# Four groups of SBUF tiles start at another byte of their 128-byte line

## The reference

```python
# layer 0, three rounds: gated recurrent update
a_in = a_out = adj @ h;  av = concat(a_in, a_out)
z = sigmoid(lin(av, w3) + lin(h, u3));  r = sigmoid(lin(av, w4) + lin(h, u3))
hv = tanh(lin(av, w5) + lin(r * h, u5));  h = (1 - z) * h + z * hv
# layer 1: attention without softmax
q, k, v = x @ Wq.T, x @ Wk.T, x @ Wv.T
rel = adjacency.T * (q @ k.T);  rel = rel / norm(rel, axis=2);  out = rel @ v
# layer 2
out = (adj @ x) @ weight + bias
# layer 3, norm_adj = adj scaled by the inverse roots of its row sums on both sides
out = norm_adj @ (x @ weight) + bias
```

## The kernel before, in words

| byte in the line | tiles |
|---|---|
| 0 | w34T, w4T, w5T, u3T, u5T, wvT, wqk, ident, adj_nat; all of the states hf and hb; all of both lanes (a, gate, rh, z, kept, cand); x_front, input_t |
| 32 | adjT, norm_adjT, w2s, w3s, sum, rel (an empty tile of 32 bytes, `shift_32`, stands ahead of them) |
| 64 | normed, result, v, sq_sum (behind `shift_back`) |

## Time and profile before

### The profile page before, as it was taken

The page is one execution under the profiler, slowest core; times in us unless marked ns, Lnnn a source line. Parts: engine busy times, 40 slices in busy tenths (PEclk is TensorE's granted clock), DMA queues, the critical chain, the costliest instruction groups (busy, mean ns, idle before and its releaser), DMA issues.

```text
span 1212.9 us, 21243 instructions
## 1 busy us (share of the span) xinstructions
PE 1198.3 (99%) x7454; PEld 1079.2 (89%) x7454; DVE 1002.6 (83%) x2220; ACT 655.7 (54%) x1179; POOL 191.7 (16%) x447
## 2 busy tenths in 40 slices
PE   9999999999999999999999999999999999999997
PEld 8789899898988989899898998989889898998896
DVE  7689788897878879788897888978789797885898
ACT  5455555555555555555555555555555555554442
POOL 1002021110211203012020211102111030120022
PEclk9999999999999999999999999999999999999998
DMA  6030221303113030220302213031130302200001
GB/s 209 18 88 18 70 71 35 104 0 88 50 35 104 0 104 35 52 87 14 107 17 69 69 35 104 0 87 52 35 104 0 104 35 51 87 12 24 1 2 35
DMA packets 105021, 66.93 MB, mean 55 GB/s; under 512 B 65690, under 2 KB 98468, under 8 KB 104996
## 3 DMA queue, kind: packets, MB, share of 16 engines
q1 hardware_dynamic: 104784, 66.08, 18.2%
q0 software_dynamic: 192, 0.52, 0.2%
q10 hardware_dynamic: 20, 0.01, 0.0%
HBM read 35.13 MB, written 23.07 MB: 48 GB/s over the span
## 4 chain that ended last, share of the span: by engine, by line
PE 97%; DVE 2%; POOL 0%; ACT 0%; issue 0%; DVEq 0%; POOLq 0%
PE b_ps L520 41%; PE f_ps L520 32%; PE f_ps L515 15%; PE b_ps L515 7%; PE f_ps L682 1%; PE b_ps L746 1%; PE b_ps L564 0%; PE f_ps L1057 0%; DVE f_stats L1683 0%; DVE hf_feat L1699 0%; DVE f_gate L1699 0%; DVE b_rh_lo L1725 0%; PE b_ps L579 0%; DVE b_ps L1720 0%; PE f_ps L589 0%
## 5 line engine op out<-in xcount | busy, mean ns | idle before, releaser
L428 POOL TENSOR_TENSOR b_var_eps<-b_moments,eps 128x2 f32<-128x2 f32 x120 | 34.7, 289 | 904.2 <-DVE b_moments L1690 904.2
L1120 ACT ACTIVATE f_cand<-f_ps,bias_c 128x512 f32<-128x512 f32 x66 | 45.4, 689 | 85.2 <-PE f_ps L520 85.2
L430 POOL TENSOR_TENSOR b_rstd<-b_var_eps,neg_half 128x2 f32<-128x2 f32 x120 | 88.0, 733 | 9.4
L1068 ACT ACTIVATE b_rh_hi<-b_ps 128x512 fp32r<-128x512 f32 x90 | 53.6, 596 | 63.0 <-PE b_ps L520 62.9
L1108 ACT ACTIVATE f_gate<-f_ps,bias_r 128x512 f32<-128x512 f32 x66 | 45.3, 686 | 71.0 <-PE f_ps L520 71.0
L1068 ACT ACTIVATE b_a_hi<-normed 128x512 fp32r<-128x512 f32 x60 | 37.8, 630 | 60.0 <-DVE normed L1699 60.0
L520 PE MATMUL f_ps<-adjT_hi,hf_node_hi 128*128 128x256 f32 x264 | 66.4, 285 | 0.0
L520 PE MATMUL f_ps<-adjT_lo,hf_node_hi 128*128 128x256 f32 x264 | 65.0, 280 | 0.0
L1582 DVE TENSOR_TENSOR f_cand<-f_z,f_cand 128x512 f32<-128x512 f32 x66 | 45.4, 688 | 23.0 <-ACT f_cand L1120 22.9
L1725 DVE TENSOR_TENSOR b_rh_lo<-b_ps,b_rh_hi 128x512 fp32r<-128x512 f32 x90 | 61.1, 679 | 4.0 <-ACT b_rh_hi L1068 3.9
L1566 DVE TENSOR_TENSOR f_gate<-f_gate,hf_feat 128x512 f32<-128x512 f32 x66 | 44.7, 678 | 20.0 <-ACT f_gate L1108 20.0
(11 more groups left out here) (340 smaller groups left out, 4304.4 us busy)
## 6 DMA issues: line engine op xcount, KB each, us to landing
x_front<-in_x SPq DMA_DIRECT2D x16, 512.0 KB, 3.9
x_blocks<-in_x SPq DMA_DIRECT2D x60, 128.0 KB, 2.9
input_t<-hf_feat SPq DMA_DIRECT2D x15, 512.0 KB, 3.0
turn_sum<-normed SPq DMA_DIRECT2D x14, 512.0 KB, 2.7
result<-turn_sum SPq DMA_DIRECT2D x56, 128.0 KB, 2.9
turn_f<-f_gate SPq DMA_DIRECT2D x14, 512.0 KB, 2.7
f_z<-turn_f SPq DMA_DIRECT2D x56, 128.0 KB, 2.8
out<-result SPq DMA_DIRECT2D x14, 512.0 KB, 3.2
```

Source lines behind the costliest of these rows:

```text
L428: pool.tensor_tensor(Y.var_eps[:, g], Y.moments[:, g, :, 1], eps[:], ALU.add).then_inc(Y.s_var, 1)
L430: pool.tensor_tensor(Y.rstd[:, g], Y.var_eps[:, g], neg_half[:], ALU.pow).then_inc(Y.s_rstd, 1)
L1068: return act.activation(dst, src, ACT.Copy)
L1120: act.activation(L.cand[:, k], L.ps1[:, k], ACT.Tanh, bias=bias_c[:, k:k + 1]).then_inc(L.s_tanh, 1)
```

## The change

Empty tiles of 64 bytes ([P, 16] in float32) are allocated ahead of four pairs of tiles, and another 64 bytes behind each pair. The pairs are: `rh_hi`, `rh_lo` of each lane, `wvT_hi`, `wvT_lo`, and the four tiles of `w2s` and `w3s`. So rh and wvT start at byte 64 of a line (before: 0), w2s and w3s at byte 96 (before: 32). All other tiles keep their byte within the line, though those behind a pair stand 128, 256, 384 or 512 bytes further on. No instruction is added, removed or reordered; nothing reads or writes the empty tiles.

```diff
@@ class Lane
         self.gate = sb(f"{name}_gate", full)
+        sb(f"{name}_half_line", [P, 16])
         self.rh_hi, self.rh_lo = sb(f"{name}_rh_hi", full, F32R), sb(f"{name}_rh_lo", full, F32R)
+        sb(f"{name}_half_line_back", [P, 16])
         self.z = sb(f"{name}_z", full)
@@ build
         u5T = split_matrix("u5T")
+        sb("half_line_v", [P, 16])
         wvT = split_matrix("wvT")
+        sb("half_line_v_back", [P, 16])
         wqk = split_matrix("wqk")
@@ build
         norm_adjT = split_matrix("norm_adjT")
+        sb("half_line_w", [P, 16])
         w2s = split_matrix("w2s")
         w3s = split_matrix("w3s")
+        sb("half_line_w_back", [P, 16])
```

## The result

The change makes the kernel slower. The median of its 4 runs is 1226.38 us (1225.23 to 1226.55); the kernel before, run beside it, had 1214.81 (1214.09 to 1216.31). The ratio is 1.0094, 95% interval 1.0079 to 1.0109: 11.6 us, or 0.95%. The forecast was 1213.8 us with a range up to 1218.2, so the result lies outside the range, on the side that had 0.15.

The account below looks back on a forecast made before the run. TensorE was taken as the bound, computing for 99% of the span. Terms -0.97 + 0.13 + 0 + 0 = -0.84 us took 1214.77 to 1213.93, against the median 1213.8 us; range 1211.5 to 1218.2.

Parts of the forecast that it names:

- the side that had 0.15: Whole kernel: slower by over 0.2%, needing over 1217.1 us; chance 0.15.
- placement plays no part: Rival for all matmuls: rates come from which products stand next to each other, not addresses; 1214.6 us, chance 0.08.
- the definition of the lead: All matmuls: moving tile's place within a 128-byte line less that of the tile loaded beside it sets a surcharge.
- a sign of this kind: Changed profile: groups keeping their places, as adjT against node tiles, changing over a nanosecond would show the prediction wrong.
- the 5.0 ns of the earlier trace: First matmuls after a change of shape or lead: an upset beat costs 5 ns on each of six, 0.03 us.
- Step 3, reset states: f_rh and b_rh against u5T, 576 matmuls going from lead 0 to 64: 0, bounds 7.7 us gained, 4.4 lost.
- lead 64 breaks the settled beat: Rival at reset states against u5T and what follows: 3.6 us slower, 1218.2 us; chance 0.18.
- seams: Where adjT, norm_adjT or a layer matrix meets another tile: some 79 matmuls from lead 32 to 96, 0.13 us lost.
- Step 1, keys and values: wvT and keys in b_rh against the sum, lead 96 to 32: about 690 matmuls gain 0.97 us.
- The surcharge, one for both shapes: Matmuls cost columns at 2.4 GHz plus, while a load runs, 13.3 ns at lead 0, 10.0 at 32, 11.7 at 96.
- the three prices: 13.3, 10.0 and 11.7 ns at leads 0, 32 and 96, said with the counts to cover nearly all the span.
- Step 2, layer matrices: w2s and w3s against b_rh stay at lead 32: nothing if only the lead counts; 0.13 us lost at seams.

Follow-up runs that it names:

- e4: Kernel before plus 128 empty bytes ahead of each pair and none behind, so every tile keeps its byte in the 128-byte line: 1227.70 us, 1.0107.
- e6: Kernel before plus one empty tile of 128 bytes between u5T and wvT: 1228.24 us, 1.0106.
- e5: Kernel before plus one empty tile of 256 bytes between u5T and wvT: 1214.95 us, 0.9999.
- e7: Kernel before plus an empty tile of 128 bytes ahead of all others, moving every place and no distance: 1214.89 us, 0.9998.
- e8: Changed kernel with 192 bytes instead of 64 behind each pair, so all other tiles keep their place modulo 256: 1218.45 us, 1.0022 against the kernel before.
- e11: Kernel before plus one empty tile of 64 bytes between u5T and wvT: 1219.79 us, 1.0039.
- e9: Changed kernel with 192 bytes behind each pair, and wvT's front pad put ahead of u5T, so u5T moves with the reset states: 1217.43 us, 1.0017 against before.
- e15: Kernel before with pads moving only the sum and wqk 64 bytes earlier in their line, others keeping their place modulo 256: 1213.22 us, 0.9981.
- e10: Kernel before plus one empty tile of 32 bytes between u5T and wvT: 1229.63 us, 1.0120.
- e12: Kernel before plus one empty tile of 224 bytes between u5T and wvT: 1230.34 us, 1.0132.
- e3: Kernel before plus only the pads around w2s and w3s: 1217.46 us, 1.0027.
- e1: Kernel before plus only the pads around rh of both lanes, in the class Lane: 1225.58 us, 1.0082.

## Why the prediction was wrong

**What held.** TensorE bounds the kernel, so a nanosecond of a matmul goes into the end; the busy time rose by 11.3 us and the time by 11.6. The waits and the other engines don't take part, and the clock only outside the loop, where its two stretches nearly cancel (1.6 us for after, 1.1 us for before); the loop alone gives 11.0 us. Matmuls of one shape cost by where the moving tile stands against the one loaded beside it: e4 and e6 add only whole lines of empty bytes and lose over 12 us. The rival *placement plays no part* is dead. The Trainium skill, "SBUF — State Buffer", section "Who interferes with whom", calls TensorE's two read ports, for the moving operand and for weight loads, independent. The runs don't agree if that is taken to mean that the places of the two tiles don't matter: they have 512-column matmuls of one form at 226.7 and at 233.3 ns, and only the distance has changed. Whether TensorE ever waits for another engine's access they don't test.

**The step that failed: the definition of the lead.** By it the tiles that moved by whole lines were taken to cost nothing. The prediction put it as "the place of the moving tile within a 128-byte line less that of the tile being loaded beside it", and from that took "all that is moved keeps its place in the line except four kinds of tile", at no cost. The period is 256 bytes: 128 between the tiles costs what e6 shows, 256 nothing (e5), 128 ahead of both nothing (e7). In the changed kernel f_a, hf_feat and hb_feat are 128 off their matrices, and b_a, behind one more pair of pads, is back. The price is shown without any half line in e4. Its size in the change is 11.6 less the 3.3 of e8: 8.3 us, with each median taken against its own before. The starts in the loop alone give 11.02 - 3.40 = 7.6: f_a 3.75, adjT and norm_adjT 1.12, hf_feat 0.80, keys and values 0.59, w2s and w3s 0.57, f_rh 0.34, the keys' product 0.24, v 0.15. hb_feat adds nothing to it: in the loop it pays 0.55 at lead 128 in the changed kernel and 0.56 at lead 0 in e8.

The prediction had named a sign of this kind: groups whose tiles keep their places, adjT against node tiles, changing by more than a nanosecond. In the changed kernel adjT against hb_node takes 117.8 ns each in the loop, before 116.7. The lead of these two is 32 in both, modulo 256 as well. The keys are a second such case, 117.8 ns at lead 32 in the changed kernel and 116.6 at the same lead in e8, and w2s a third: 116.7 before, 117.4 in e5 and 117.6 in e7, where nothing has changed modulo 256. So one lead can hold a whole stage of twenty-four at more than one rate. What ran ahead of the stage is the likely cause; no run has it by itself.

The trace of before could not show the period. All its large tiles agree modulo 256 where they agree modulo 128, so that the earlier trace rows fit either. The working treated the 128 as given by rows, where it was only consistent with them. It should have had the other period among its bounds: 1764 matmuls of f_a, hf_feat and hb_feat at an unknown lead, at the 5.0 ns of the earlier trace rows, are 8.8 us. That number was in reach.

**Step 3, reset states, taken as 0.** Wrong, and the rival *lead 64 breaks the settled beat* was right for the kernel that it costed: it forecast 3.6 us net of the keys' gain, e8 measured 3.3. Its parts came out less exactly: reset states 2.2 us where 2.9 were forecast, the stages behind them (f_a, hf_feat, hb_feat) 2.0 where 1.5 were; and lead 64 does settle, at 228.9 ns (e11). In the changed kernel itself f_rh stands at 192 modulo 256, not at 64. The value 0 rested on two matmuls of the earlier trace rows, 225 ns each as printed. One matmul at a new lead out of a settled beat tells nothing of the next twelve. e9 shows it from the other side: only the seams are off, the first two matmuls of b_rh's stage take 228 and 229 ns, and the next two 233 and 236.

**Step 1, keys and values,** had the right size where the rest is undisturbed: 0.97 forecast, 1.09 in e8 and 1.11 in e15. In the changed kernel only 0.31 was left.

**The surcharge, one for both shapes.** The working read 13.3, 10.0 and 11.7 ns off 256 columns, set the second 256 columns of a 512-column matmul at their bare 2.4 GHz, and priced 512 columns at other leads by that (3.3 x 576 as the price of lead 32). It fits at lead 0 only: over 213.3 ns, which is 512 columns at 2.4 GHz, the runs have 13.3 ns at lead 0, 20.0 at 32 and at 224 (e10, e12). That no load runs beside the second half isn't shown either: the profile's loads last 187 to 188 ns of the 226.7. And the three prices times the counts of the working give 1109 us, 91% of the span, not nearly all of it.

**Step 2, layer matrices,** "nothing, if only the lead counts". Modulo 256 w2s against b_rh goes from lead 32 to 160, not to 32. Measured +0.41 us for w2s and w3s, or +0.80 in the loop alone, where 0.13 was forecast for seams.

**The sum.** Forecast -0.84. Measured +11.6, which e8 parts in two: 3.3 for the half lines with the keys' gain in it, and by difference 8.3 for the whole lines.

**Open.** What in the hardware makes the period and the beat isn't settled by these runs; they show the price by distance only. No run takes the other engines' reads and writes away; that they play no part in the rates is argued, not shown. That the other tile is the one loaded for the next matmul, and not the matmul's own, is an assumption: within a stage the two are the same matrix. Distances finer than 32 bytes, and 160 at 512 columns, weren't tried. For 256 columns these are the means over stages of twenty-four in the loop: 116.6 to 117.8 at lead 32 (keys, w2s, adjT against hb_node; 118.3 for the last in e3), 117.2 to 117.6 at 160, no clear difference from 32 (w2s in the changed kernel and in e4, keys in e1), 118.3 at 224 (the keys before), 119.7 to 120.0 at 96 (w2s in e1 and e3, keys in e3 and e4); lead 0 has 120.0 in the closing part alone, and 64, 128 and 192 have no long stretch.

## What to carry to other kernels

When TensorE is the bound and weights are loaded beside each matmul, note for every pair of moving and loading tile the distance modulo 256 bytes before a tile is inserted or dropped; an empty or new tile whose size is not a multiple of 256 shifts the distance of all pairs that it stands between. To improve one pair, move the tile that the fewest other stages use, and pad to a whole 256 behind it, so that no other distance changes. Then measure the stages behind the moved tile's too: they can lose their beat with no distance of their own changed. And a period read from a trace in which all cases agree with a longer one too is a guess: price it at the longer one as well.

## What the runs showed of the hardware that was not expected

- 128 empty bytes between two groups of tiles cost 13 us of 1215 (e6), 224 cost 15 (e12), and 256 cost nothing (e5). It is the distance between tiles, not their place: 128 ahead of everything is free (e7).
- For 512 columns the price by distance is not gradual: 226.7 ns at 0, 228.9 at 64, and 232.3 to 233.3 at 32, 96, 128, 192 and 224. At 512 columns distance 0 is the cheapest. At 256 columns 0 and 96 are the dearest of the five with long stretches (120.0, against 116.7 at 32 in most of them).
- The rate has a memory: a single matmul at another distance at each end keeps a stage of twelve at 230.1 ns that would run at 226.7 (e9, b_rh against u5T; the mean from starts). A stage with no distance changed even at its ends went from 228.5 to 231.8 ns (e8, hb_feat against u3T).
